# Reading two accumulators back one after the other, and moving four of eight adds from GpSimd to VectorE

## The reference, cut to what matters

```python
x = x + _L0_xattn_ref(_layernorm(x), ..., ctx_2048, ctx_2048, wq, wk, wv, wo)
x = x + _L0_ffn_ref(_layernorm(x), w_gate, wi_0, wi_1, wo)        # 8 experts, 2 for each row
x = x + _L1_xattn_ref(_layernorm(x), ctx_2048, mask_BxS2_bk0)     # scores, mask, softmax, readout
x = x + _L1_ffn_ref(_layernorm(x), gate_w, w_gate, w_up, w_down)  # 32 experts, 8 for each row
```

## Time and profile before

| | |
|---|---|
| median of three runs | 1076.29 us |
| the profiled execution | 1073.37 us |
| its span | 1071.6 us |
| granted TensorE clock, mean | 0.908 |
| busy: PE, VectorE, ScalarE, GpSimd | 76%, 48%, 49%, 47% |
| on the chain that ended last: PE / DMA / issue | 39% / 15% / 14% |
| loads back from the accumulators | 32 of 256 KB, on SyncE's queue |
| scatters that add | 100, on GpSimd's queue |

### The profile page before, as it was taken

One profiled execution on the slowest core, in us unless ns is written; L12 is line 12 of the kernel. 1 busy time (PEld: TensorE's weight loads), 2 busy tenths in 40 slices (PEclk: granted clock), 3 DMA queues, 4 the chain that ended last, 5 costly groups with the idle time before them and its releaser, 6 DMA issues.

```text
span 1071.6 us, 20434 instructions
## 1 busy us (share of the span) xinstructions
PE 811.7 (76%) x5206; PEld 441.1 (41%) x5207; DVE 515.7 (48%) x1523; ACT 524.3 (49%) x782; POOL 499.5 (47%) x413
## 2 busy tenths in 40 slices
PE   4998999997389993769871377878877778777770
PEld 3444455544244442335341243444444444444440
DVE  5653444564435533557763243544545435353432
ACT  5532334544356741345452165556756556555550
POOL 4880001001346755004575555566766556656560
PEclk9999999998589996979985698999999999989995
DMA  8553010000348958301110358878987878779668
GB/s 283 168 182 118 11 40 21 31 30 31 111 126 217 236 101 240 129 30 41 41 42 23 108 129 234 194 165 195 242 221 191 228 165 199 186 169 233 150 111 254
DMA packets 108391, 150.73 MB, mean 141 GB/s; under 512 B 18336, under 2 KB 59552, under 8 KB 108352
## 3 DMA queue, kind: packets, MB, share of 16 engines
q0 software_dynamic: 25760, 56.56, 26.9%
q1 hardware_dynamic: 80000, 93.49, 26.6%
q10 hardware_dynamic: 2592, 0.19, 0.2%
HBM read 107.34 MB, written 42.86 MB: 140 GB/s over the span
## 4 chain that ended last, share of the span: by engine, by line
PE 39%; DMA 15%; issue 14%; DVE 10%; DVEq 8%; ACT 5%; SPq 3%; POOL 3%; ACTq 2%; POOLq 0%; another core or an unknown queue 0%
PE pst L187 32%; DMA mid<-moe_normalised_rows,small 6%; DMA big<-in_L_ffn_w_down_dram 4%; DMA x_rows<-mid,small 3%; DVEq L1160 3%; DVEq L1154 2%; PE pst L1264 2%; PE pst L493 2%; POOL moe_tokens_of_experts L994 1%; DVE big L1146 1%; DMA big<-x_rows 1%; ACTq L1154 1%; DVE mid L1385 1%; DMA big<-in_L_ffn_wo_dram 1%; PE pst L953 1%
## 5 line engine op out<-in xcount | busy, mean ns | idle before, releaser
L187 PE MATMUL pst<-big,mid 128*128 (+1 forms) x1392 | 287.0, 359 | 22.1 <-DVE mid L1377 10.4
L1460 POOL DMA_INDIRECT x_rows<-mid,small x100 | 160.1, 1601 | 130.9 <-ACT mid L1321 77.0
L994 POOL DMA_INDIRECT moe_tokens_of_experts<-token_no,small x80 | 82.8, 1035 | 285.4 <-DVE small L1047 264.9
L187 PEld LDWEIGHTS pst<-big,mid 128*128 128x128 f16 x1392 | 137.8, 102 | 137.1 <-issue 47.6
L1450 POOL DMA_INDIRECT mid<-moe_normalised_rows,small x106 | 114.7, 1082 | 97.4 <-DVE small L1367 37.4
L1264 PE MATMUL pst<-big,mid 128*128 x520 | 132.3, 388 | 1.4 <-ACT mid L1313 0.9
L1302 ACT ACTIVATE mid<-pst 128x1024 f16<-128x1024 f16 x102 | 103.7, 1017 | 55.7 <-PE pst L1236 44.0
L1377 DVE SCALAR_TENSOR_TENSOR mid<-pst,small,mid 128x192 f32<-128x192 f32 (+1 forms) x100 | 42.6, 426 | 119.8 <-ACT mid L1308 87.8
L1236 PE MATMUL pst<-id,mid 128*128 128x128 f16 x816 | 66.5, 228 | 39.0 <-DMA mid<-moe_normalised_rows,small 34.5
L187 PE MATMUL pst<-ctxN,mid 128*128 128x512 f16 x384 | 88.6, 389 | 3.2 <-ACT mid L619 3.2
L1321 ACT ACTIVATE mid<-pst 128x512 f32<-128x512 f32 x100 | 59.9, 599 | 58.0 <-PE pst L1264 46.0
(11 more groups left out here) (201 smaller groups left out, 1193.4 us busy)
## 6 DMA issues: line engine op xcount, KB each, us to landing
big<-in_L_ffn_w_gate_dram SPq DMA_DIRECT2D x32, 384.0 KB
big<-in_L_ffn_w_up_dram SPq DMA_DIRECT2D x32, 384.0 KB
big<-in_L_ffn_wi_dram SPq DMA_DIRECT2D x16, 512.0 KB
big<-in_L_ffn_w_down_dram SPq DMA_DIRECT2D x32, 256.0 KB
big<-in_L_ffn_w_down_dram SPq DMA_DIRECT2D x64, 128.0 KB
moe_normalised_rows<-xn SPq DMA_DIRECT2D x18, 256.0 KB, 2.0
mid<-in_ctx_dram SPq DMA_DIRECT2D x16, 256.0 KB, 4.3
big<-in_ctx_turned_dram SPq DMA_DIRECT2D x16, 256.0 KB, 4.6
```

The costliest lines, as they stand in the source:

```text
L187: last = nc.tensor.matmul(dst, stationary(a, c), moving(b, c), start=(k == 0), stop=(k == 3 * len(parts) - 1))
L994: nc.gpsimd.indirect_dma_start(out=self.tab_d[:, :], out_offset=bass.IndirectOffsetOnAxis(ap=self.addr[j % 2][:, k:k + 1], axis=0), in_=to ...
L1460: nc.gpsimd.indirect_dma_start(out=acc_d[p][:, :], out_offset=bass.IndirectOffsetOnAxis(ap=self.si[p], axis=0), in_=self.y[p], in_offset=N ...
```

## The change

The accumulators are now read back one after the other: `done` is raised twice, first when accumulator 0's last scatter has landed, then when accumulator 1's and the gathers have. SyncE issues the eight loads of accumulator 0 behind the first and the eight of accumulator 1 behind the second. In the middle VectorE sums tiles 0 to 3 and GpSimd tiles 4 to 7, with a semaphore each; `norm2.normalise(0)` moves out of `attn1.dve` to behind the sums of tiles 0 and 1, then come the sums of tiles 2 and 3, and the mask's maximum and flag behind these. VectorE waits for the second `done` before it makes the mask's bias.

```diff
             def normalise(self, dve, pair):
                 tiles = (2 * pair, 2 * pair + 1)
-                dve.wait_ge(back_s, tiles[-1] + 1)
+                if pair < 2:
+                    dve.wait_ge(back_s, tiles[-1] + 1)
+                else:
+                    dve.wait_ge(back_pool_s, tiles[-1] + 1 - SUMS)
@@ Attention.dve
-                if not self.first:
-                    norm2.normalise(dve, 0)
@@ Experts.pool
-                for p in range(2):
-                    pool.wait_ge(self.scat[p], 16 * (np_ + 1))
+                pool.wait_ge(self.scat[0], 16 * (np_ + 1))
+                pool.sem_inc(self.done, 1)
+                pool.wait_ge(self.scat[1], 16 * (np_ + 1))
                 pool.wait_ge(self.xg_in[0], 16 * (np_ + 2))
                 pool.wait_ge(self.xg_in[1], 16 * (np_ + 1))
                 pool.sem_inc(self.done, 1)
@@
+        back_pool_s = sem("x_summed_by_gpsimd")
+        SUMS = NT // 2
+        def sums_back(sp, done):
+            sp.wait_ge(done, 1)
             for i in range(NT):
                 sp.dma_start(x_sb[:, i, :], acc_d[0][i * P:(i + 1) * P, :]).then_inc(x_in_s[i], 16)
+            sp.wait_ge(done, 2)
+            for i in range(NT):
                 sp.dma_start(part[:, i, :], acc_d[1][i * P:(i + 1) * P, :]).then_inc(x_in_s[i], 16)
+        def sum_up(dve, i, loaded):
+            dve.wait_ge(x_in_s[i], loaded)
+            nc.vector.tensor_tensor(x_sb[:, i, :], x_sb[:, i, :], part[:, i, :], ALU.add).then_inc(back_s, 1)
@@ SyncE, the middle
-            sp.wait_ge(back_s, NT)
+            sp.wait_ge(back_s, SUMS)
+            sp.wait_ge(back_pool_s, NT - SUMS)
@@ SyncE, the end
-                sp.wait_ge(back_s, NT + i + 1)
+                sp.wait_ge(back_s, SUMS + i + 1)
@@ GpSimd, the middle
-            for i in range(NT):
+            for i in range(SUMS, NT):
                 pool.wait_ge(x_in_s[i], 48)
@@ VectorE, the middle and the end
-            dve.wait_ge(exp0.done, 1)
+            dve.wait_ge(exp0.done, 2)
             link(dve, nc.vector.tensor_scalar(mbias, mraw, 1.0, NEG, ALU.subtract, ALU.mult))
+            for i in range(2):
+                sum_up(dve, i, 48)
+            norm2.normalise(dve, 0)
+            for i in range(2, SUMS):
+                sum_up(dve, i, 48)
             link(dve, nc.vector.tensor_reduce(mval, mbias, AX_X, ALU.max))
             link(dve, nc.vector.tensor_scalar(mval, mval, -0.5, None, ALU.is_ge))
             attn1.dve(dve)
             exp1.dve(dve)
             for i in range(NT):
-                dve.wait_ge(x_in_s[i], 80)
-                nc.vector.tensor_tensor(x_sb[:, i, :], x_sb[:, i, :], part[:, i, :], ALU.add).then_inc(back_s, 1)
+                sum_up(dve, i, 80)
```

More of the change, by code:

```diff
@@ L1508, in program @@
         back_s = sem("x_summed")
-        def sums_back(sp):
+        back_pool_s = sem("x_summed_by_gpsimd")
+        SUMS = NT // 2
+        def sums_back(sp, done):
+            sp.wait_ge(done, 1)
             for i in range(NT):
                 sp.dma_start(x_sb[:, i, :], acc_d[0][i * P:(i + 1) * P, :]).then_inc(x_in_s[i], 16)
+            sp.wait_ge(done, 2)
+            for i in range(NT):
                 sp.dma_start(part[:, i, :], acc_d[1][i * P:(i + 1) * P, :]).then_inc(x_in_s[i], 16)
+        def sum_up(dve, i, loaded):
+            dve.wait_ge(x_in_s[i], loaded)
+            nc.vector.tensor_tensor(x_sb[:, i, :], x_sb[:, i, :], part[:, i, :], ALU.add).then_inc(back_s, 1)
         block = ctx.enter_context(nc.Block())
@@ L1526, in _ @@
                 sp.dma_start(mraw[:, b, :], mask_in[b, :].partition_broadcast(P)).then_inc(g_in_s, 16)
-            sp.wait_ge(exp0.done, 1)
-            sums_back(sp)
+            sums_back(sp, exp0.done)
             exp1.blank_sp(sp)
             exp1.sp_first(sp)
-            sp.wait_ge(back_s, NT)
+            sp.wait_ge(back_s, SUMS)
+            sp.wait_ge(back_pool_s, NT - SUMS)
             sp.wait_ge(zero_s, 2)
@@ L1536, in _ @@
             exp1.sp(sp)
-            sp.wait_ge(exp1.done, 1)
-            sums_back(sp)
+            sums_back(sp, exp1.done)
             ot = out.rearrange("b (t p) d -> p (b t) d", p=P)
             for i in range(NT):
-                sp.wait_ge(back_s, NT + i + 1)
+                sp.wait_ge(back_s, SUMS + i + 1)
                 sp.dma_start(ot[:, i, :], x_sb[:, i, :]).then_inc(out_s, 16)
@@ L1554, in _ @@
             nc.gpsimd.memset(zero, 0.0).then_inc(zero_s, 1)
-            for i in range(NT):
+            for i in range(SUMS, NT):
                 pool.wait_ge(x_in_s[i], 48)
-                nc.gpsimd.tensor_tensor(x_sb[:, i, :], x_sb[:, i, :], part[:, i, :], ALU.add).then_inc(back_s, 1)
+                nc.gpsimd.tensor_tensor(x_sb[:, i, :], x_sb[:, i, :], part[:, i, :], ALU.add).then_inc(back_pool_s, 1)
             for j in range(NT):
```

## The result

| | before | after |
|---|---|---|
| median (runs) | 1078.06 us (4) | 1066.58 us (4) |
| lowest, highest | 1075.6, 1081.84 | 1063.06, 1069.13 |
| profiled execution, its span | 1073.37, 1071.6 | 1069.13, 1067.4 |

A fourth run of the kernel before, 1081.84 us, has joined the three. The ratio is 0.9888, 95% interval 0.9839 to 0.9937: faster by 1.1%, 11.5 us between the medians, where 2 us were forecast. Rival A, the fastest of my cases, had 1069.6 us, which is still 3 us too many.

The account below looks back on a forecast made before the run. It took the middle as bound by one load's landing, the end by bytes. Middle +2.4 - 0.6 - 2.15 = -0.35, end -1.9, together -2.25 us: 1076.29 - 2.25 = 1074.0 us, range 1068.8 to 1079.3.

Parts of the forecast that it names:

- Rival A: Middle and end: the early start keeps nearly all its worth, -6.65 us together, 1069.6 us; chance 0.15.
- the sum itself: Whole kernel: middle -0.35 us plus end -1.9 us gives -2.25 us, 1074.0 us.
- What bounds the kernel now: Middle bound by the landing of tile 1's load from accumulator 1, end by 6.3 MB of loads and stores.
- The earlier start: SyncE's first load goes earlier by 3.0 us in the middle and by 3.2 at the end.
- What the scatter takes from the loads: Middle and end: the last scatter beside the early loads costs the lead 1.3 us, between 0.65 and 2.1.
- rival B: Middle and end: the last scatter lands only when the eight loads have, +1.4 us, 1077.7 us; chance 0.15.
- The queue's order in the middle: Tile 1's awaited load, now tenth instead of fourth, lands 2.4 us later, bounds +1.75 and +3.2.
- My sign of being wrong: Middle: statistics earlier than 12.4 us behind the last scatter would mean the queue is not what bounds the middle.
- VectorE's adds: Middle: VectorE adds tiles 0 and 1 in 0.69 us each instead of 1.27, -0.6 us.
- VectorE's stream beside GpSimd: Middle: statistics and normalising, stretched while GpSimd adds, keep their length: 0 us, bounds -1.3 and 0.
- The clock: Middle: TensorE's pause shrinks from 2.71 to 0.4 us and full clock holds through the scores, -2.15 us.
- The mask's maximum, the wait for the second step, SyncE's zeros: Middle: all cost nothing; sums, maximum and flag, 4.7 us, hide in VectorE's 7.57 us gap before the scores.

Follow-up runs that it names:

- e_pad_dve5: Kernel before (uint16 expert table) plus five unused semaphore increments in VectorE's stream ahead of the second stage's loop: 1070.32 against 1076.58 us, ratio 0.9936.
- the seven runs with 4 to 64 increments: Kernel before (uint16 table) with 4, 5, 8, 13, 16, 32 or 64 unused increments in VectorE's stream ahead of the loop: ratios 0.9933 to 0.9959.
- e_end: Kernel before (uint16 table) with only the end's two-step done and accumulators read back in turn, middle unchanged: 1072.42 against 1076.58 us, ratio 0.9960.
- e_pad_behind5: Kernel before with five unused increments in VectorE's stream behind the second stage's loop: 1073.64 against 1073.59 us, ratio 0.9997.
- a_pad_pool4: Changed kernel (uint16 table) with four unused increments in GpSimd's stream, putting its loop back where it stood before: 1066.40 us, ratio 0.9899 to the kernel before.
- the reordered loads: Changed kernel (uint16 table), tile 1's accumulator 1 load sixth in the middle's queue, not tenth: ratios to the kernel before 0.9877 and 0.9886 in two runs.
- e_mid: Kernel before (uint16 table) with only the middle of the change, loops shifted as in the changed kernel, end unchanged: 1071.42 us, ratio 0.9940.

## Why the prediction was wrong

**The step that failed is the sum itself: it has no term for code that the change leaves alone.** "What bounds the kernel now" looked at the two places of the edit, and "the change part by part" counted the instructions moved between engines only by their time, never by what they do to the places of those behind them. VectorE's stream became 5 instructions longer, which took 0.22 us out of each of some 40 passes (bare head 848 and 631 ns). The forecast was -0.2% and the result -1.1%; of the 0.9 points between them the place of the loop is 0.64 by `e_pad_dve5` (0.55 on the mean of the seven runs with 4 to 64 increments), and the rest is the end (-0.40% by `e_end`, interval 0.17 to 0.64, where -1.9 us, or 0.18%, were forecast). `e_pad_behind5` and the edge between 2 and 4 show that it is the place; `a_pad_pool4` that it is VectorE's and not GpSimd's. The trace shows where in the head the time goes, 0.1 us at the jump and 0.1 us at one fixed place of the program, and not what the queue does in these pauses; the cause of the pauses stays open. The Trainium skill, in "Runtime: NRT & Kernel Launch", section "Instruction fetch mechanics", says that instructions are fetched in blocks of 256 and that a taken branch whose target lies outside the window held costs a stall. The runs fit a block's boundary within the first few of the loop's some 65 instructions, which 4 or more then leave behind for good: the pause moves two instructions forward with a shift of 2 and is gone with 4. No run shows the fetching, and none moved the loop on to the next boundary.

**The earlier start: right, a little low at the end.** 3.0 us were forecast in the middle and 3.2 at the end. Measured from the last scatter's issue: 4.82 - 1.73 = 3.1, and 5.02 - 1.47 = 3.55.

**What the scatter takes from the loads: too high, within its bounds.** 1.3 us were taken between 0.65 and 2.1. In the one pair of profiles above, the first load to the end of the last add grew by 0.2 us; over all of them it is 14.5 us on the mean of the twelve with the old end (14.1 to 15.0) and 15.3 on the mean of the eight with the new one (14.8 to 16.4), 0.8 us more. The old end starts slowly (145 and 268 GB/s in its first four microseconds of loads), and with the loads beside the scatter that start falls into the scatter's time, which may be why the price is low; no run separates it. So the end was worth 3.5 - 0.8 = 2.7 us in the profiles and 0.40% (1.8 to 6.9 us) in the times of `e_end`, and not 1.9: between the forecast and rival A's 3.2. The Trainium skill, in "DMA: Bandwidth & Descriptors", section "Queues, rings and completion order", has the engines alternate between the queues, and the prediction worked out from it that both kinds of work would simply add up, 2.1 us. The traces contradict that sum here, for a scatter whose rows take so much longer than their bytes: even the largest of the eight values lies only 1.9 us above the old mean. The scatter's own landing was late by 0.3 us (5.08 against 4.78) in the first pair and by 0.5 on the mean (4.9 to 5.7 us in the eight, 4.7 to 4.9 in the twelve), so rival B, where it is held up until the loads are through, did not happen.

**The queue's order in the middle: right in kind, too high in size.** +2.4 us were forecast for the tenth load. In the first pair it landed at most 0.5 us later against the last scatter: the ninth at 10.73 us, the tenth no later than 11.5 (the second add's start), against 10.99 for the fourth before. In the five profiles with the changed middle the second add starts 11.9 us behind the last scatter on the mean (11.4 to 12.3). From the first load to the landing of the tenth the forecast had 10.31 + 1.3 = 11.6 us; it was at most 9.7 in the first pair and at most 10.1 on the mean of the five, less than the 10.31 of the end alone. My sign of being wrong, statistics earlier than 12.4 us, came true by 0.24 us in the first profile, but it does not mean what I wrote there: the reordered loads show that the place in the queue costs about 1.5 us.

**VectorE's adds: right.** Two adds take 1.30 us and the statistics follow at once. They stand 12.57 us behind the last scatter on the mean of the five, 12.41 on the mean of the thirteen profiles with the old middle: the same within their spread (a standard deviation of 0.35 us each), where 1.8 later were forecast.

**VectorE's stream beside GpSimd: wrong.** I put it at 0, between -1.3 and 0, since GpSimd, starting with tile 4, "still overlaps". It overlaps more: the two instructions of line 320 take 2.42 us in all five profiles with the changed middle and 1.5 to 2.0 in the thirteen with the old one. That is +0.9 us, outside the bounds, and it opens the second pause below.

**The clock: wrong in the profile, and no steady gain.** -2.15 us were forecast. The pause before the first transpositions did shrink, from 2.71 to 0.40 us, but a second pause of 0.76 us came between the two tiles' transpositions, and the scores again started at half clock. From the scores' start to their first use it took 8.4, 7.2, 7.0, 7.2 and 5.5 us in the five profiles with the changed middle and 6.8 to 8.3 in those with the old one: about 0.6 us less on the mean. Only in the one with 5.5 us (`e_mid`) was the granted clock at its full level from the start to the end of the scores, as forecast, and why in that one is open. The middle as a whole, from the last scatter to the first use of the scores, is 27.1 us on the mean of the five (25.9 to 28.1) against 27.5 of the thirteen (26.1 to 28.6). That this is the -0.35 us of the forecast is luck: it is less than the spread, and it comes from a queue and a clock that were both wrong.

**The mask's maximum, the wait for the second step, SyncE's zeros: right.** The maximum ran from 426.81 to 429.30 in VectorE's gap, which still had 4.86 us left. The flag took 0.17 us and not 1.03, now that GpSimd does not add beside it.

**The range and the bound.** The measured median lies 2.2 us below the range. Its lower end lay near A's time, whose parts all came from the two places; nothing in it stood for the rest of the kernel.

## What to carry to other kernels

When an edit moves instructions between engines ahead of a loop with jumps, cut both traces at events that both have (here the scatters) before believing that the edit explains the difference; then put the same number of idle instructions in the kernel before, in front of the loop and behind it, as a control. Here that control was worth more (0.64%) than what the edit did by itself (0.40%). And where a last transfer is slow for another reason than its bytes, start the independent loads beside it, with the load that somebody waits for near the front.

## What the runs showed of the hardware that I had not expected

- The place of a loop of some 65 instructions in VectorE's stream was worth 0.22 us in each pass and 0.6% of the kernel: slow with a shift of 0 and 2 instructions, fast with 4 to 64.
- Loads of 256 KB beside an adding scatter cost the scatter 0.5 us on the mean and themselves 0.8; of the 2.1 us of engine time at 54 to 77 GB/s that the scatter showed alone, most was not capacity in use.
- VectorE's instructions beside GpSimd's adds were stretched: a tensor_scalar of 128x512 took 1.49 us in place of 0.53.
- One chip of those used ran the kernel before in 1059.7 us where the others took 1073 to 1078. From the last scatter of the first stage to the first of the second the four kernels profiled there took 209 to 212 us, all others 223 to 228 and one 233; their loops were like the others'. The cause is open.
